# Another order of the same instructions in the repeated iteration of a two-layer attention kernel, on all five engines

## The chip, the cores and the metric

The kernel runs on one core of one Trainium2 chip. The metric is device time in microseconds (us) from launch to end, median over runs. A profiled execution also has a span, from its first to its last instruction, which is a little shorter than its time.

## The reference, cut to what matters

For each of 32 batch entries `x` (128 channels x 512 positions) and `ctx` (the same shape), two layers:

```
# layer 0: position attention, 512 x 512 energies, divided by column sums
energy = (w_qk @ ctx).T @ (w_qk @ x);  a = softmax(energy, -1);  a = a / (1e-7 + a.sum(1))
x_r = (w_v @ x + b_v) @ a
x1  = x + relu(w_t @ (x - x_r) + b_t)
# layer 1: grouped-query attention, 128 x 128 scores, 32 query heads, 8 key heads of 16
q, k, v = x1 @ Wq + bq, ctx @ Wk + bk, ctx @ Wv + bv
p = softmax(q k.T / 4 + mask);  out = (p v) @ Wo + bo
y = layernorm(out + x1) * gamma + beta
```

Everything is float32. The mask given is zero, and a flag computed at run time lets the kernel leave out its additions.

## The kernel before, in words

The batch is worked in 16 pairs; `j` (0, 1) is the entry within a pair. To keep float32 accuracy at the matmul rate of the rounded format, an operand is split in a high part (`..h`) and a low part (`..l`), and a product is three matmuls (high x high, high x low, low x high). The high part is written by ScalarE, or by GpSimd for `xs` and `ys`; the low part by VectorE or GpSimd.

The pairs are software-pipelined in four stages. Iteration `i` holds stage 0 of pair i+1 (`z_project`: the Gram matrix of `w_qk` times x), stage 1 of pair i (layer 0, and keys and values), stage 2 of pair q = i-1 (queries, maxima, scores, exponentials, weighted values) and stage 3 of pair i-2 (output projection, layer norm, store). Iterations 1, 2 and 15 run the same function `iteration` with some stages left out, 3 to 14 are a hardware loop with all of them; "a turn" below is one pass of that loop. Iteration 0 and the tail of the last pair have functions of their own.

Each engine's order of instructions is written out by hand in its own `iteration`, one for SyncE's DMA queue (from L471), GpSimd (L681), TensorE (L958), ScalarE (L1269) and VectorE (L1673). Engines meet only at counting semaphores: `wait(engine, name, i, n)` waits for the n-th signal of that name in iteration i. An instruction behind a waiting one on its engine waits too.

The 8 PSUM banks form a ring. `WIDE_USES` lists the uses of an iteration in TensorE's order (72 places, two of them "skip", so 9 times round), and a use gets the bank that the use 8 places before it had; `wait_slot` makes TensorE wait for the signal in `RELEASE` that says that use has been read. So moving a use in the order also changes whose reader it waits for. The names: `en` energies, `tva` the two layer-0 projections of x, `b` the attended sums, `z`, `q`, `k`, `v`, `vt` (transposed v), `mx` (scores from which the row maxima are taken), `m` (the maxima spread), `st` (transposed scores), `o` (weighted values), `r` (x1 transposed for the residual), `wo` (output projection).

The part that couples the engines most closely runs once per turn:

1. TensorE's four `max_scores` (L895) follow the four `q_project` (L871 to L873). VectorE reads each of the 16 banks with one `score_max` (L1567), then `max_split` (L1577 to L1582) writes `mrow`.
2. TensorE's `max_spread` (L910) turns `mrow` into bank `m`, VectorE's `max_rows` (L1588) copies it into `mrep`, and a DMA (`stack_maxima`, L413) puts it into `qstack` rows 96 and up.
3. TensorE's first `scores` (L924) waits for that DMA (`maxrow_in`), since the maxima are subtracted by the matmul itself.

SyncE issues in this stretch: 8 transfers of `qh` (L403) when the fourth `q_high` is done, 4 of `ql` (L407), the load of the next `ys` (`next_y`, L377), then the one of `mrep`. Later in the iteration stand the load of `et` (`next_et`, L383), the gathering of softmax denominators and values across partitions (L420, L425), the stores (L393), 12 transfers of `kstack` (`stack_k`, L434), and at the head of the next iteration the loads of `xt` (L380) and `xs` (L374).

At the end of an iteration VectorE inverts the denominators (`inverse_denominators`, L1592), weighs (`weigh_out`, L1598) and finishes layer 0 for j = 1 (`layer0_out`: L1531, L1534, four of L1537 and one of L1543, which writes `x2` and waits for TensorE's `residual_transpose` of the pair before, L881, for it reads the old `x2`). `x2_high` (ScalarE, L1205) and `x2_low` (GpSimd, L669) split it for the queries of the next iteration.

## Time and profile before

| what | value |
|---|---|
| median of 3 runs | 782.83 us (782.27 to 787.34) |
| profiled execution, its own time | 782.72 us |
| its span | 780.3 us |
| mean granted TensorE clock | 0.980 |
| TensorE matmul busy | 716.9 us, 92% |
| VectorE busy | 608.3 us, 78% |
| ScalarE busy | 463.5 us, 59% |
| GpSimd busy | 582.2 us, 75% |
| DMA | 101.64 MB, queue 1 takes 43.6% of 16 engines |

Busy shares tell how full an engine is, not which one sets the end. For that one reads the chain of waits (what released the last instruction, and what released that one, back to the start), and the instructions in order of time around each wait. A wait is shown at the engine that waited, with the instruction or DMA whose signal came last. For DMAs the queue's rows give the time of issue only; from issue to landing is read from the chain.

### The profile page before, as it was taken

How to read it: one execution, taken by the hardware profiler on the slowest of the kernel's cores; microseconds unless marked ns; L12 is line 12 of the kernel's file. 1: busy time of each engine (PE TensorE's matmuls, PEld its weight loads, DVE VectorE, ACT ScalarE, POOL GpSimd, SP SyncE). 2: the span in 40 equal slices, each digit the busy share in tenths (PEclk: the TensorE clock that was granted, in tenths of full speed). 3: DMA queues.
4: the chain of work that ended last, by engine and by line, in shares of the span. 5: the costliest groups of instructions: out<-in, count | busy, mean ns of one | idle time of the engine just before them, and what ended most of it. 6: DMA issues, size and time to landing. Idle time of an engine off the chain costs nothing.

```text
span 780.3 us, 17141 instructions
## 1 busy us (share of the span) xinstructions
PE 716.9 (92%) x4886; PEld 579.4 (74%) x4886; DVE 608.3 (78%) x1030; ACT 463.5 (59%) x1058; POOL 582.2 (75%) x752
## 2 busy tenths in 40 slices
PE   6798979999999999999999999999999999998773
PEld 5676867888788787878778787877878787775642
DVE  5675875969789796969879696978879697885747
ACT  5655638376574937657483855747385665748161
POOL 4886488697877969787896978789697878858054
PEclk9999999999999999999999999999999999999896
DMA  8544361634527262452717254362715436251511
GB/s 321 176 123 125 92 177 55 177 99 148 138 94 191 83 179 89 152 142 89 205 68 184 88 157 129 101 191 74 200 66 171 122 116 170 81 146 61 136 37 61
DMA packets 60363, 101.64 MB, mean 130 GB/s; under 512 B 10032, under 2 KB 30128, under 8 KB 60208
## 3 DMA queue, kind: packets, MB, share of 16 engines
q1 hardware_dynamic: 59616, 101.03, 43.6%
q10 hardware_dynamic: 720, 0.27, 0.2%
q8 instruction: 14, 0.23, 0.1%
q14 instruction: 13, 0.11, 0.0%
HBM read 41.50 MB, written 8.39 MB: 64 GB/s over the span
## 4 chain that ended last, share of the span: by engine, by line
PE 66%; DVE 12%; DMA 9%; issue 5%; SPq 3%; POOL 2%; ACT 1%; DVEq 1%; POOLq 0%; ACTq 0%
PE banks L924 8%; PE banks L840 7%; DMA qstack<-mrep 7%; DVE maxima L1567 6%; PE banks L937 5%; PE banks L871 4%; PE banks L873 4%; PE banks L872 4%; PE banks L895 4%; PE banks L827 2%; PE banks L825 2%; PE banks L826 2%; PE banks L813 2%; SPq L403 2%; PE banks L949 2%
## 5 line engine op out<-in xcount | busy, mean ns | idle before, releaser
L1567 DVE TENSOR_REDUCE maxima<-banks 128x4 f32<-128x512 f32 x256 | 158.9, 685 | 5.9 <-PE banks L895 4.5
L1226 ACT ACTIVATE prob<-banks 128x512 f32<-128x512 f32 x256 | 135.1, 608 | 26.3 <-PE banks L924 25.0
L1592 DVE RECIPROCAL dens<-dens 128x512 f32<-128x512 f32 x30 | 100.4, 3348 | 46.6 <-DMA dens<-sides 46.6
L601 POOL TENSOR_TENSOR ta<-ta,cb_s 128x516 f32<-128x516 f32 x64 | 77.1, 1205 | 74.9 <-ACT ta L1168 74.8
L840 PEld LDWEIGHTS banks<-ta,att 128*128 128x128 f32 x1024 | 119.0, 190 | 2.7 <-POOL ta L608 0.2
L840 PE MATMUL banks<-ta,att 128*128 128x130 f32 x1024 | 119.4, 275 | 0.0
L1160 ACT ACTIVATE att<-banks,negmax 128x512 f32<-128x512 f32 x128 | 88.7, 716 | 33.7 <-DVE negmax L1517 33.6
L1210 ACT ACTIVATE qh<-banks,bq_s 128x256 fp32r<-128x256 f32 x64 | 30.7, 480 | 104.1 <-PE banks L873 104.1
L924 PE MATMUL banks<-qstack,kstack 128*128 128x512 f32 x256 | 81.4, 422 | 9.5 <-DMA qstack<-mrep 9.2
L1517 DVE TENSOR_REDUCE negmax<-banks 128x1 f32<-128x512 f32 x128 | 85.2, 685 | 3.9 <-PE banks L827 3.7
L871 PE MATMUL banks<-x2h,wq_h 128*128 128x256 f32 x256 | 74.5, 291 | 4.1 <-POOL x2l L669 4.1
L1543 DVE SCALAR_TENSOR_TENSOR x<-ta,xt 128x512 f32<-128x512 f32 x32 | 38.4, 1199 | 44.9 <-PE banks L881 44.3
L873 PE MATMUL banks<-x2h,wq_l 128*128 128x256 f32 x256 | 72.7, 284 | 0.0
L872 PE MATMUL banks<-x2l,wq_h 128*128 128x256 f32 x256 | 72.4, 283 | 0.0
L1153 ACT ACTIVATE zh<-banks 128x512 fp32r<-128x512 f32 x32 | 19.4, 607 | 88.0 <-PE banks L804 88.0
L924 PEld LDWEIGHTS banks<-qstack,kstack 128*128 128x128 f32 x256 | 44.2, 191 | 32.1 <-issue 13.6
L937 PE MATMUL banks<-prob,v 128*32 128x512 f32 x512 | 62.0, 599 | 2.9 <-ACT prob L1226 2.9
L674 POOL TENSOR_TENSOR atl<-at,ath 128x512 fp32r<-128x512 f32 x30 | 44.8, 1494 | 26.0 <-ACT ath L1242 26.0
L871 PEld LDWEIGHTS banks<-x2h,wq_h 128*128 128x128 f32 x256 | 48.8, 191 | 6.5 <-POOL x2l L669 4.4
L949 PE MATMUL banks<-wo_h,ath 128*128 128x512 f32 x120 | 50.5, 421 | 2.5 <-POOL atl L674 1.5
L825 PE MATMUL banks<-zh,yh 128*128 128x512 f32 x128 | 51.3, 401 | 1.4 <-DVE maxima L1567 1.4
L827 PE MATMUL banks<-zh,yl 128*128 128x512 f32 x128 | 50.7, 396 | 0.0
(170 smaller groups left out, 1956.1 us busy)
## 6 DMA issues: line engine op xcount, KB each, us to landing
qstack<-qh SPq DMA_DIRECT2D x128, 128.0 KB, 2.4
xs<-in_x SPq DMA_DIRECT2D x16, 512.0 KB, 4.4
ys<-in_ctx SPq DMA_DIRECT2D x16, 512.0 KB, 3.8
et<-in_ctx_turned SPq DMA_DIRECT2D x16, 512.0 KB, 3.3
xt<-in_x_turned SPq DMA_DIRECT2D x16, 512.0 KB, 3.6
kstack<-kph SPq DMA_DIRECT2D x128, 64.0 KB, 2.0
qstack<-ql SPq DMA_DIRECT2D x64, 128.0 KB, 2.4
out_x<-late SPq DMA_DIRECT2D x32, 256.0 KB, 2.1
```

Source lines behind the costliest of these rows:

```text
L601: nc.gpsimd.tensor_tensor(part, part, cb_s[:].unsqueeze(1).broadcast_to([P, 2, CW]), ALU.add).then_inc(sem["ta_done"], 1)
L840: last = mm(o, att[:, j, n, bass.ts(m, P)], ta[:, j, n, 0:BW], start=n == 0, stop=n == KC - 1)
L871: mm(o, wq_h[:, k, g], x2h[:, k], start=k == 0, stop=False)
L872: mm(o, wq_h[:, k, g], x2l[:, k], start=False, stop=False)
L873: last = mm(o, wq_l[:, k, g], x2h[:, k], start=False, stop=k == KC - 1)
L924: last = mm(o, kstack[:, j, 2 * p + odd], qstack[:, p, j], start=True, stop=not masked)
L937: last = mm(banks[32 * p:32 * p + 32, slot(plan, name)], v2[:, j, 2 * p + odd], prob[:, 2 * p + odd], start=True, stop=True, tile_position ...
L1160: nc.scalar.activation(att[:, j, n], banks[:, slot(plan, f"en{j}{n}")], exp_f, bias=negmax[:, j, n:n + 1], accum_out=rowsum[:, j, n:n + 1] ...
L1226: nc.scalar.activation(prob[:, 2 * p + odd], banks[:, slot(plan, f"st{j}{kv}")], exp_f).then_inc(sem["prob_done"], 1)
L1517: nc.vector.tensor_reduce(negmax[:, j, n:n + 1], banks[:, slot(plan, f"en{j}{n}")], AX.X, ALU.max, negate=True).then_inc(sem["negmax_done" ...
L1567: nc.vector.tensor_reduce(maxima[:, 0, :, p, :, g].rearrange("x o j -> x j o"), banks[:, slot(plan, f"mx{g}{p}")].rearrange("x (j o s) -> ...
L1592: nc.vector.reciprocal(dens[:], dens[:]).then_inc(sem["dinv_done"], 1)
```

## The change: the same instructions, another order

No instruction is added or taken out, and no shape, SBUF tile or semaphore changes. In the function `iteration` of each engine some calls change places, and `WIDE_USES` is written anew to follow TensorE's order, so that many uses take another bank and wait for another reader.

```diff
--- before.py
+++ after.py
@@ -77,15 +77,15 @@
...
 WIDE_USES = (
-    ("tva00", 1), ("en00", 1), ("en01", 1), ("en02", 1), ("en03", 1), ("en10", 1), ("wo0", 3), ("tva01", 1),
-    ("tva02", 1), ("q0", 2), ("q1", 2), ("mx00", 2), ("mx01", 2), ("mx02", 2), ("mx03", 2), ("tva03", 1),
-    ("q2", 2), ("tva10", 1), ("tva11", 1), ("mx10", 2), ("mx11", 2), ("mx12", 2), ("mx13", 2), ("q3", 2),
-    ("tva12", 1), ("tva13", 1), ("mx20", 2), ("mx21", 2), ("mx22", 2), ("mx23", 2), ("mx30", 2), ("mx31", 2),
-    ("mx32", 2), ("mx33", 2), ("wo1", 3), ("skip", 1), ("skip", 1), ("en11", 1), ("en12", 1), ("m", 2),
-    ("z0", 0), ("en13", 1), ("b00", 1), ("b01", 1), ("st00", 2), ("st01", 2), ("st02", 2), ("st03", 2),
-    ("st04", 2), ("k", 1), ("st05", 2), ("st06", 2), ("st07", 2), ("z1", 0), ("r0", 2), ("o00", 2), ("o01", 2),
-    ("st10", 2), ("st11", 2), ("st12", 2), ("st13", 2), ("v", 1), ("st14", 2), ("st15", 2), ("b10", 1),
-    ("b11", 1), ("st16", 2), ("r1", 2), ("st17", 2), ("o10", 2), ("o11", 2), ("vt", 1),
+    ("en00", 1), ("en01", 1), ("tva00", 1), ("tva01", 1), ("en02", 1), ("en03", 1), ("en10", 1), ("tva02", 1),
+    ("wo0", 3), ("q0", 2), ("q1", 2), ("mx00", 2), ("mx01", 2), ("mx02", 2), ("mx03", 2), ("tva03", 1), ("q2", 2),
+    ("mx10", 2), ("mx11", 2), ("mx12", 2), ("mx13", 2), ("tva10", 1), ("tva11", 1), ("q3", 2), ("tva12", 1),
+    ("tva13", 1), ("mx20", 2), ("mx21", 2), ("mx22", 2), ("mx23", 2), ("mx30", 2), ("mx31", 2), ("mx32", 2),
+    ("mx33", 2), ("wo1", 3), ("skip", 1), ("en11", 1), ("en12", 1), ("z0", 0), ("en13", 1), ("skip", 1), ("m", 2),
+    ("b00", 1), ("b01", 1), ("st00", 2), ("st01", 2), ("st02", 2), ("st03", 2), ("st04", 2), ("st05", 2), ("k", 1),
+    ("st06", 2), ("st07", 2), ("z1", 0), ("r0", 2), ("o00", 2), ("o01", 2), ("st10", 2), ("st11", 2), ("st12", 2),
+    ("v", 1), ("st13", 2), ("st14", 2), ("st15", 2), ("b10", 1), ("b11", 1), ("st16", 2), ("vt", 1), ("st17", 2),
+    ("o10", 2), ("o11", 2), ("r1", 2),
 )
...
@@ -470,33 +470,31 @@
...
                 q = i - 1
-                if s1:
-                    this_xt(i)
                 if load_next:
                     next_x(i)
+                if s1:
+                    this_xt(i)
                 if s2:
...
                     stack_maxima(q)
+                    gather_denominators(q, 0)
+                    gather_values(q, 0)
+                    gather_denominators(q, 1)
+                if s1:
+                    next_mask(i)
+                if s3:
+                    store(i - 2, 0)
+                if s2:
+                    gather_values(q, 1)
                 if load_next:
                     next_et(i)
-                if s2:
-                    gather_denominators(q, 0)
-                    gather_values(q, 0)
-                if s3:
-                    store(i - 2, 0)
-                if s2:
-                    gather_denominators(q, 1)
-                if s1:
-                    next_mask(i)
-                if s2:
-                    gather_values(q, 1)
-                if s1:
-                    stack_k(i)
                 if s3:
                     store(i - 2, 1)
+                if s1:
+                    stack_k(i)
 
...
@@ -686,16 +684,19 @@
...
                     add_bias(i, 0, 0)
-                    add_bias(i, 0, 1)
                 if s3:
...
                 if s1:
-                    scale_values(i, 0)
+                    add_bias(i, 0, 1)
                     add_bias(i, 1, 0)
-                    add_bias(i, 1, 1)
                 if split_next:
                     split_x(i + 1, 0)
+                if s1:
+                    scale_values(i, 0)
+                if split_next:
                     split_x(i + 1, 1)
+                if s1:
+                    add_bias(i, 1, 1)
                 if s3:
...
@@ -704,14 +705,14 @@
...
                     scale_values(i, 1)
-                    spread_k(i)
-                if s2:
-                    residual_bias(q, 0)
                 if s3:
                     scale_shift(i - 2, 0)
+                if s1:
+                    spread_k(i)
                 if s3 and (s1 or s2):
...
                 if s2:
+                    residual_bias(q, 0)
                     at_low(q, 0)
...
@@ -958,17 +959,16 @@
...
                 if s1:
-                    tva_project(i, plan, 0, 0)
                     energy(i, plan, 0, 0)
                     energy(i, plan, 0, 1)
+                    tva_project(i, plan, 0, 0)
+                    tva_project(i, plan, 0, 1)
                     energy(i, plan, 0, 2)
...
                     energy(i, plan, 1, 0)
+                    tva_project(i, plan, 0, 2)
                 if s3:
                     out_project(i - 2, plan, i, 0)
-                if s1:
-                    tva_project(i, plan, 0, 1)
-                    tva_project(i, plan, 0, 2)
                 if s2:
...
@@ -977,11 +977,11 @@
...
                     q_project(q, plan, i, 2)
+                    max_scores(q, plan, i, 1, masked)
                 if s1:
...
                 if s2:
-                    max_scores(q, plan, i, 1, masked)
                     q_project(q, plan, i, 3)
...
@@ -994,12 +994,12 @@
...
                     energy(i, plan, 1, 2)
-                if s2:
-                    max_spread(q, plan, i)
                 if s0:
...
                     energy(i, plan, 1, 3)
+                if s2:
+                    max_spread(q, plan, i)
                 if s1:
...
@@ -1009,10 +1009,10 @@
...
                     scores(q, plan, i, 0, 4, masked)
+                    scores(q, plan, i, 0, 5, masked)
                 if s1:
...
                 if s2:
-                    scores(q, plan, i, 0, 5, masked)
                     scores(q, plan, i, 0, 6, masked)
...
@@ -1024,10 +1024,10 @@
...
                     scores(q, plan, i, 1, 2, masked)
+                if s1:
+                    kv_project(i, plan, "v", 1, "v_ps")
+                if s2:
                     scores(q, plan, i, 1, 3, masked)
-                if s1:
-                    kv_project(i, plan, "v", 1, "v_ps")
-                if s2:
                     scores(q, plan, i, 1, 4, masked)
...
@@ -1035,12 +1035,13 @@
...
                     scores(q, plan, i, 1, 6, masked)
-                    residual_transpose(q, plan, i, 1)
+                if s1:
+                    v_transpose(i, plan)
+                if s2:
                     scores(q, plan, i, 1, 7, masked)
...
                     values(q, plan, i, 1, 1)
-                if s1:
-                    v_transpose(i, plan)
+                    residual_transpose(q, plan, i, 1)
 
...
@@ -1268,31 +1269,31 @@
...
                 q = i - 1
-                if s2:
-                    x2_high(q, 1)
+                if s1:
+                    tva_raw(i, plan, 0, 0)
+                    tva_raw(i, plan, 0, 1)
                 if weights:
                     out_weights_high()
+                if s2:
+                    x2_high(q, 1)
                 if s1:
                     exp_energy(i, plan, 0, 0)
-                    tva_raw(i, plan, 0, 0)
                     exp_energy(i, plan, 0, 1)
+                    tva_raw(i, plan, 0, 2)
                     exp_energy(i, plan, 0, 2)
...
                     exp_energy(i, plan, 1, 0)
-                    tva_raw(i, plan, 0, 1)
-                    tva_raw(i, plan, 0, 2)
                 if s2:
...
                     at_high(i - 2, 1)
+                if s2:
+                    q_high(q, plan, 2)
                 if s1:
                     tva_raw(i, plan, 0, 3)
-                if s2:
-                    q_high(q, plan, 2)
-                if s1:
                     tva_raw(i, plan, 1, 0)
...
@@ -1315,39 +1316,43 @@
...
                     exp_scores(q, plan, 0, 6)
+                if s1:
+                    k_high(i, plan)
+                if s2:
                     exp_scores(q, plan, 0, 7)
-                if s1:
-                    k_high(i, plan)
+                if s3:
+                    normalise(i - 2, 0)
+                if s2:
+                    keep_sums(q, plan, 0, 0)
                 if s0:
...
                 if s2:
-                    keep_sums(q, plan, 0, 0)
                     keep_sums(q, plan, 0, 1)
-                if s3:
-                    normalise(i - 2, 0)
-                if s2:
+                    exp_scores(q, plan, 1, 0)
                     residual(q, plan, 0)
...
                 if s2:
-                    exp_scores(q, plan, 1, 0)
                     exp_scores(q, plan, 1, 1)
                     exp_scores(q, plan, 1, 2)
+                if s3 and (s1 or s2):
+                    normalise(i - 2, 1)
+                if s1:
+                    x2_high(i, 0)
+                if s2:
                     exp_scores(q, plan, 1, 3)
                     exp_scores(q, plan, 1, 4)
-                if s3 and (s1 or s2):
-                    normalise(i - 2, 1)
-                if s2:
                     exp_scores(q, plan, 1, 5)
...
                     keep_sums(q, plan, 1, 0)
+                if s1:
+                    v_place(i, plan, 0)
+                if s2:
+                    keep_sums(q, plan, 1, 1)
                     at_high(q, 0)
-                    keep_sums(q, plan, 1, 1)
                     residual(q, plan, 1)
                 if s1:
-                    x2_high(i, 0)
-                    v_place(i, plan, 0)
                     v_place(i, plan, 1)
...
@@ -1682,12 +1687,11 @@
...
                     energy_max(i, plan, 1, 0)
+                    row_inverse(i, 0)
                 if s3:
...
                     q_low(q, plan, 0)
-                if s1:
-                    row_inverse(i, 0)
                 if s3:
...
@@ -1696,9 +1700,9 @@
...
                     score_max(q, plan, 0, 3)
-                    q_low(q, plan, 2)
                     score_max(q, plan, 1, 0)
                     score_max(q, plan, 1, 1)
+                    q_low(q, plan, 2)
                     score_max(q, plan, 1, 2)
...
@@ -1710,26 +1714,28 @@
...
                     score_max(q, plan, 3, 3)
+                if s3:
+                    residual_add(i - 2, plan, 1)
+                if s2:
                     max_split(q)
                 if s3:
-                    residual_add(i - 2, plan, 1)
                     row_statistics(i - 2, 1)
...
                     energy_max(i, plan, 1, 1)
+                if s0:
+                    z_low(i, plan, 0)
                 if s2:
                     max_rows(q, plan)
+                if s1:
+                    energy_max(i, plan, 1, 2)
                 if s3:
...
                 if s1:
-                    energy_max(i, plan, 1, 2)
                     energy_max(i, plan, 1, 3)
                     ctx_low(i)
-                if s0:
-                    z_low(i, plan, 0)
-                if s1:
-                    row_inverse(i, 1)
                     layer0_out(i, plan, 0)
                     k_low(i, plan)
+                    row_inverse(i, 1)
                 if s0:
...
```

## Rows read from the trace of the kernel before

**Rows 1.** The page: TensorE's busy time, and the chain's shares by engine.

```profile
PE 716.9 (92%) x4886; PEld 579.4 (74%) x4886; DVE 608.3 (78%) x1030; ACT 463.5 (59%) x1058; POOL 582.2 (75%) x752
...
PE 66%; DVE 12%; DMA 9%; issue 5%; SPq 3%; POOL 2%; ACT 1%; DVEq 1%; POOLq 0%; ACTq 0%
```

**Rows 2.** Windows view, one turn: length, busy us (instructions) per engine, clock, DMA, GB/s.

```profile
473.31:518.40 45.09, 43.95 (x307) 35.76 (x306) 36.85 (x61) 28.18 (x66) 36.67 (x49) 1.00 0.46 132
```

**Rows 3.** TensorE in order of time, same turn: start, us, instruction, idle before it.

```profile
477.12 1.42 PE L924 MATMUL banks<-qstack,kstack 128*128 128x512 f32 x5 [0.38 <-DMA qstack<-mrep]
...
493.19 0.36 PE L813 MATMUL banks<-cw_h,xh 128*128 128x258 f32 x1
...
500.59 0.28 PE L871 MATMUL banks<-x2h,wq_h 128*128 128x256 f32 x1
...
516.39 0.33 PE L910 MATMUL banks<-ident_r,mrow 128*128 128x128 f32 x1 [0.61 <-DVE mrow L1582]
```

**Rows 4.** Chain that ended last, same turn: start us, us, what.

```profile
473.31 3.58 DMA qstack<-mrep
...
477.12 1.42 PE banks L924 x5
...
493.43 0.12 PE banks L813
...
493.79 0.23 PE banks L825
...
503.62 0.66 PE banks L895 x8
...
511.75 3.68 DVE maxima L1567 x6
...
516.17 0.69 DVE late L1604
...
518.17 0.21 DVE mrep L1588
...
518.40 3.52 DMA qstack<-mrep
```

**Rows 5.** SyncE's queue in order of time, same turn (issue time alone).

```profile
506.05 0.35 SPq L380 DMA_DIRECT2D xt<-in_x_turned  x1
506.70 0.39 SPq L374 DMA_DIRECT2D xs<-in_x  x1
510.01 5.03 SPq L403 DMA_DIRECT2D qstack<-qh  x8
515.09 2.50 SPq L407 DMA_DIRECT2D qstack<-ql  x4
517.68 0.53 SPq L377 DMA_DIRECT2D ys<-in_ctx  x1
```

**Rows 6.** Chain, iteration 15, in which no ys is loaded.

```profile
698.99 2.48 DMA qstack<-mrep
```

**Rows 7.** VectorE in order of time, same turn as Rows 3.

```profile
477.25 0.68 DVE L1511 TENSOR_TENSOR zl<-banks,zh 128x512 fp32r<-128x512 f32 x1
...
492.04 1.13 DVE L1537 SCALAR_TENSOR_TENSOR ta<-banks,colinv,ta 128x128 f32<-128x128 f32 x4
493.20 1.58 DVE L1543 SCALAR_TENSOR_TENSOR x<-ta,xt 128x512 f32<-128x512 f32 x1
```

**Rows 8.** ScalarE in order of time, same turn.

```profile
492.27 0.60 ACT L1236 ACTIVATE sides<-banks 128x512 f32<-128x512 f32 x1 [0.43 <-PE banks L937]
...
494.76 0.58 ACT L1199 ACTIVATE v<-banks 128x64 f32<-128x64 f32 x4
```

**Rows 9.** GpSimd in order of time, same turn.

```profile
498.40 1.30 POOL L669 TENSOR_TENSOR x2l<-x,x2h 128x512 fp32r<-128x512 f32 x1
```

**Rows 10.** Chain, iteration 2.

```profile
109.57 5.00 DMA qstack<-mrep
```

**Rows 11.** SyncE's queue, iteration 2.

```profile
112.11 0.35 SPq L383 DMA_DIRECT2D et<-in_ctx_turned  x1
```

More of the change, by code:

```diff
@@ L472, in iteration @@
                 q = i - 1
+                if load_next:
+                    next_x(i)
                 if s1:
                     this_xt(i)
-                if load_next:
-                    next_x(i)
                 if s2:
@@ L490, in iteration @@
                 if s2:
-                    gather_denominators(q, 1)
-                if s1:
-                    next_mask(i)
-                if s2:
                     gather_values(q, 1)
+                if load_next:
+                    next_et(i)
+                if s3:
+                    store(i - 2, 1)
                 if s1:
                     stack_k(i)
-                if s3:
-                    store(i - 2, 1)
             def first_iteration(i, load_next, s1, s2, s3, setup=False):
@@ L1026, in iteration @@
                     scores(q, plan, i, 1, 2, masked)
-                    scores(q, plan, i, 1, 3, masked)
                 if s1:
@@ L1030, in iteration @@
                 if s2:
+                    scores(q, plan, i, 1, 3, masked)
                     scores(q, plan, i, 1, 4, masked)
@@ L1295, in iteration @@
                 if s1:
+                    tva_raw(i, plan, 0, 3)
                     tva_raw(i, plan, 1, 0)
```

9 lines of the change are left out of this document (3 added, 6 removed).

## The prediction

> **What bounds the kernel now.** I read the page first. TensorE is busy 92% of the span and has 66% of the chain of waits; the next is VectorE with 12%, then DMA with 9% [rows 1]. So TensorE is near the bound, and the question is what its remaining waits hang on. Then one turn of the loop: it takes 45.09 us, of which TensorE is busy 43.95 [rows 2]. At most 1.14 us a turn can be won by order alone, 13.7 us over 12 turns. TensorE in order of time shows where most of it lies: 0.61 us ahead of `max_spread`, which waits for `mrow`, and 0.38 us ahead of the first `scores`, which waits for the transfer of `mrep` [rows 3].
>
> The chain shows which of these repeats the turn. From the first scores at 477.12 it stays on TensorE to the first `max_scores` at 503.62, then runs through VectorE's 16 maxima, `residual_add`, `max_rows`, and ends in the transfer of `mrep`, 3.52 us, after which the next scores begin [rows 4]. SyncE's queue gives a second road to the same place: 8 issues of `qh` from 510.01 (5.03 us), 4 of `ql` (2.50 us), `ys` at 517.68, and only behind it `mrep` at 518.40 [rows 4, 5]. The queue starts that series when the fourth query projection has been copied, so this road too starts at TensorE and ends at `mrep`.
>
> Which road binds is told by the transfer itself. Issued at 473.31 it takes 3.58 us [rows 4]. In iteration 15, where no `ys` goes ahead of it, it takes 2.48 us [rows 6]. The 1.10 us between them is time behind `ys`. The landing is thus set by when `ys` was issued, and `mrep` could be issued up to about 1.1 us later for the same landing.
>
> **The change part by part.** The sum goes against the profiled execution's own 782.72 us, 0.11 us under the median of 782.83, so no correction is needed.
>
> *TensorE, `max_spread` behind `z_project` 0 and `energy(1,3)`.* Six matmuls of 512 columns, 0.23 us apart [rows 4], or 1.4 us, now fill the 0.61 us wait [rows 3]; the wait ahead of `max_spread` goes. But TensorE reaches the scores that much earlier and they still wait for `mrep`. If the landing stays, the 0.38 us becomes 0.99 us and the turn keeps its length: 0.
>
> *VectorE, `z_low` 0 ahead of `max_rows`; `residual_add` 1 ahead of `max_split` instead of behind it.* `residual_add` already stands between the last maximum and `max_rows`, at 516.17 [rows 4], so `mrep` does not see it; only `mrow` comes 0.69 us later, and TensorE has the 1.4 us to cover that. `z_low` is new on this path: 0.68 us [rows 7]. So `mrep` is issued at most 0.68 us later. Bounds: nothing, if the landing hangs on `ys` (1.10 us of slack, 0.42 left), and +0.68 x 12 = +8.2 us if the transfer's time runs from its own issue. I take 0, since rows 4 and 6 are the same transfer with and without `ys` ahead. Below nothing is excluded: even an earlier `mrep` would be behind `ys`.
>
> The Trainium skill speaks against this, in "DMA: Bandwidth & Descriptors", "Anatomy of one DMA": a DMA costs a fixed time of about 2 us plus its bytes over a bandwidth, counted from its issue. By that the later issue would be paid in full. The trace disagrees with a fixed cost here, 3.58 against 2.48 us for the same bytes.
>
> *SyncE, `xs` ahead of `xt`, `et` and one store ahead of the 12 `stack_k`.* The queue gets the issue of one 512 KB load (0.35 to 0.39 us plus a gap) ahead of `stack_k`, so `xs` and `xt`, issued at 506.70 and 506.05 now [rows 5], end some 0.4 us later as a pair, while `xs` alone is first. The queue then still waits for `qh` at 510.01, 2.9 us after the last of them: hidden. What could leak is their data being in the way of `qh`; bounds 0 and +0.4 x 12 = +4.8 us. I take 0, the queue's pause being far longer.
>
> *The seam between iterations.* TensorE now begins with `en00` where `tva00` stood at 493.19, and `en00`, `en01` take the banks of `b10`, `b11`. VectorE frees these with the four L1537 at 492.04, lasting 1.13 us [rows 7]: the second half at 492.6, the last at 493.17, needed at 493.19 and 0.69 us later. ScalarE's tail is reordered: `v_place` ended at 495.34 and had `x2_high` 0 ahead of it, which is moved 6 places up; the tail from `keep_sums` at 492.27 loses that 0.5 us and ends near 494.8 [rows 8]. `tva01` wants the bank of `vt` from it, at 493.19 + 1.39 + 0.36 = 494.94. Margins of 0.1 to 0.5 us where there were 0.5 us and more. `residual_transpose` 1 now ends the iteration; `x2` for j = 1, at 493.20 [rows 7], waits for it, and it ends at about 493.3. Then `x2_low` ends at 499.70 [rows 9] and the queries start at 500.59 [rows 3], a slack of 0.9 us that swallows small delays. Bounds: 0 and +0.7 us a turn (the `v_place` tail as late as now, 495.34, plus its signal and the delayed `x2`); nearest row is 494.8, so I take +0.1 over 13 turns: +1.3 us.
>
> *The rest* (`max_scores` 1 ahead of two `tva`, `k_high`, `normalise`, `scale_values`, `spread_k`, `row_inverse` 1, `v` one score earlier) moves work between places where the chain never passes. The sum of TensorE's work from the scores to `max_scores` 0 is the same set of matmuls. VectorE's maxima are then served no earlier. Cost 0; cover is ScalarE's and GpSimd's idle time (28.18 and 36.67 us busy of 45.09 [rows 2]); without it, up to one `score_max` or copy, 0.7 us a turn.
>
> *`et` out from behind `mrep`.* In iteration 2 `mrep` takes 5.00 us [rows 10], and the load of `et` is issued at 112.11 while it is under way [rows 11]; in the turns `mrep` takes 3.58 [rows 4]. The change puts `et` far later. Bounds 0 and -1.42 us there; iteration 1 is alike with a third of that. I take -1.4 in all, near the row. In the turns `et` follows the landing of `mrep`, and nothing is won.
>
> Sum: 782.7 + 0 + 0 + 1.3 - 1.4 = 782.6 us; I say 782.
>
> **The rivals.**
>
> *A, slower: the later `mrep` is paid.* Place: the wait of the first scores. Price 0.68 x 12 = 8.2 us, less the `et` gain: 789.5 us, and with the leak of `xt` up to 792. It decides from the point where VectorE is more than 1.1 us later than now; a late `z_high` ahead of `z_low` would do it. For: `mrep` was issued just when VectorE had it ready (518.17 + 0.21 against 518.40 [rows 4]). Against: rows 6. Chance 0.13.
>
> *B, slower: the seam.* `v_place` 1 stands behind `residual` 1, which waits for the last matmuls of the iteration; if that tail is 0.8 us later than I place it, `tva01` stops TensorE by 0.7 us: 13 x 0.7 = 9.1 us, 791 us. It decides from 0.1 us. For: thin margins. Against: ScalarE waits at 492.27 [rows 8], so the tail is short of work, not late. Chance 0.14.
>
> *C, faster: the freed wait is won.* If the landing of `mrep` moved with TensorE, the 0.61 us would be won: 0.61 x 12 = 7.3 us, and 1.4 at the start: 774.0 us. It needs the queue's series to start earlier, by smoother work ahead of the fourth query projection. Against: TensorE has no wait listed between the scores and `max_scores` 0, the chain being all matmuls there [rows 4]. Chance 0.15.
>
> *D: all is hidden*, my forecast, 0.58: 779 to 786 us.
>
> **How the numbers follow.** The likeliest case gives 782. From no change a measurement of this kernel can tell about 1%, 7.8 us: below 775.0 or above 790.7. Faster by that: most of C, 0.13. Slower: half of A, most of B, 0.19. Between: D, the rest of the others and unnamed small effects, 0.68. The range leaves out the lower part of C and the upper ends of A and B: 774 to 791.
>
> **What would show it.** Right, if in the changed kernel's turn the idle ahead of `max_spread` is gone, the idle ahead of the first scores is about 1.0 us, `mrep` is issued about 0.6 us later in the turn and takes about 2.9 us instead of 3.5, and the turn stays at 45.1 us. A would show as a transfer of still 3.5 us and a turn of 45.7; B as a wait of `en` or `tva` at the head of the turn for ScalarE or VectorE; C as a turn of 44.5 with the fourth query projection earlier after the scores. In iteration 2 `mrep` should take about 3.6 us. Wrong is the forecast if the turn moves by more than 0.3 us either way.

## The result, and the profile after

The changed kernel takes 788.01 us (median of 8 runs, 786.22 to 790.69), the kernel before 782.57 us (8 runs, 782.14 to 787.34). The ratio is 1.0057, with a 95% interval of 1.0034 to 1.0081: 5.4 us slower, inside the range of the forecast and under its bound of 1%, but it moved where the forecast said that it would not, and by more than the measurement is uncertain. The profiled execution took 789.49 us, with a span of 787.6 us.

The page of the changed kernel; the last field of the line beginning with L925 is the idle time ahead of that group of instructions and what ended it:

```profile
span 787.6 us, 17111 instructions
PE 719.1 (91%) x4886; PEld 584.2 (74%) x4886; DVE 598.9 (76%) x1030; ACT 467.6 (59%) x1058; POOL 580.8 (74%) x752
...
PE 67%; DVE 11%; DMA 9%; issue 6%; POOL 3%; SPq 2%; ACT 1%; DVEq 1%; POOLq 0%
...
L925 PE MATMUL banks<-qstack,kstack 128*128 128x512 f32 x256 | 81.4, 424 | 23.3 <-DMA qstack<-mrep 23.3
```

The chain's shares have hardly moved against [rows 1]. What has moved is the wait ahead of the scores: 23.3 us over 15 waits, where the kernel before has 9.2 us. Part of it is no new wait: the 0.61 us a turn that stood ahead of `max_spread` [rows 3] now stands here.

First the loop's steady part, in the turn that answers to [rows 2, 3]. TensorE in order of time, and the windows view of the same turn:

```profile
521.17 0.40 PE L828 MATMUL banks<-zh,yl 128*128 128x512 f32 x1
521.41 0.22 PE L911 MATMUL banks<-ident_r,mrow 128*128 128x128 f32 x1
521.47 3.79 PE L841 MATMUL banks<-ta,att 128*128 128x130 f32 x32
526.50 1.61 PE L925 MATMUL banks<-qstack,kstack 128*128 128x512 f32 x6 [1.24 <-DMA qstack<-mrep]
```

```profile
core 0: us, PE busy (x) PEld busy (x) DVE busy (x) ACT busy (x) POOL busy (x), PEclk, DMA share, GB/s
481.53:526.50 44.97, 43.71 (x306) 35.77 (x306) 35.83 (x61) 28.48 (x65) 36.54 (x48) 1.00 0.46 133
```

`max_spread` (L911) follows its neighbour with no wait, the scores wait 1.24 us instead of 0.38, and the turn is 44.97 us long against 45.09. Over the turns 5 to 14 the wait is 1.13 to 1.59 us, so this is one of the shorter ones, and the turns are 45.13 us long on average, against 45.10. The chain of waits shows `z_low` now in front of `max_rows`, and SyncE's queue shows `ys` where it was:

```profile
522.26 0.68 DVE zl L1516
522.94 0.21 DVE mrep L1593
...
523.17 3.08 DMA qstack<-mrep
```

```profile
522.09 0.53 SPq L377 DMA_DIRECT2D ys<-in_ctx  x1
523.17 0.64 SPq L413 DMA_DIRECT2D qstack<-mrep  x1
```

From the first scores `ys` is issued after 40.56 us in both kernels (477.12 to 517.68 [rows 3, 5], 481.53 to 522.09 here). `mrep` is issued 1.08 us behind `ys` instead of 0.72, and lands 4.16 us after the issue of `ys` instead of 4.24 (518.40 + 3.52 less 517.68 [rows 4, 5]). The later issue is paid back by the shorter transfer.

So the loss is not in the steady turn. The table cuts the span at the landings of `mrep` (issue plus transfer time in each chain of waits). Iteration n's landing is the end of that transfer in iteration n; the last column but one is the last pair's landing, in the tail. The two lower rows are repeats of both kernels in one later session, described as experiments below.

| kernel | landing, iteration 1 | 1 to 4 | 4 to 14 | 14 to 15 | 15 to last pair | rest | span |
|---|---|---|---|---|---|---|---|
| before | 67.0 | 139.4 | 451.0 | 44.1 | 41.9 | 36.9 | 780.3 |
| changed | 69.9 | 140.5 | 451.3 | 44.5 | 44.2 | 37.2 | 787.6 |
| before, repeated | 67.1 | 135.3 | 451.2 | 44.2 | 42.3 | 37.3 | 777.5 |
| changed, repeated | 68.8 | 142.0 | 451.9 | 43.7 | 43.3 | 37.4 | 787.0 |

The ten turns that make up 57% of the span differ by 0.3 and 0.7 us. The rest is in the first iteration (+2.9, +1.7), the next three (+1.1, +6.7) and the last pair (+2.3, +1.0). One profile of each kernel can't give these shares: the same kernel differs from itself by up to 4.1 us in iterations 1 to 4.

**Iteration 1.** ScalarE of the changed kernel in order of time, then the same engine of the kernel before:

```profile
44.06 0.88 ACT L1169 ACTIVATE ta<-banks 128x258 f32<-128x258 f32 x2 [4.94 <-PE banks L816]
44.83 1.91 ACT L1268 ACTIVATE wo_h<-prob 128x2048 fp32r<-128x2048 f32 x1
46.64 0.62 ACT L1206 ACTIVATE x2h<-x 128x512 fp32r<-128x512 f32 x1
```

```profile
38.37 0.63 ACT L1205 ACTIVATE x2h<-x 128x512 fp32r<-128x512 f32 x1 [0.28 <-DVE x L1543]
38.90 1.89 ACT L1267 ACTIVATE wo_h<-prob 128x2048 fp32r<-128x2048 f32 x1
```

TensorE of the changed kernel, where its instructions of iteration 1 begin and where the queries begin:

```profile
40.62 0.62 PE L826 MATMUL banks<-zh,yh 128*128 128x512 f32 x1 [4.01 <-issue]
...
48.71 0.38 PE L872 MATMUL banks<-x2h,wq_h 128*128 128x256 f32 x1 [1.77 <-POOL x2l L667]
```

In iteration 1 TensorE starts its function late, after 4.01 us of issue (3.21 us in the kernel before). The changed ScalarE puts two `tva_raw` and the copy `wo_h` ahead of `x2_high` 1; the `tva_raw` have to wait for TensorE, so `x2_high` falls from 38.37 to 46.64. GpSimd's `x2_low` follows at 47.39, and the queries wait 1.77 us for it. In the steady turn the queries show no such wait.

**Iterations 2 to 4.** The waits of the changed TensorE ahead of the first scores in iterations 1 to 4, and the windows view behind the first, the second and around the third of them (the clock is the third field from the right):

```profile
70.12 1.75 PE L925 MATMUL banks<-qstack,kstack 128*128 128x512 f32 x6 [1.94 <-DMA qstack<-mrep]
117.47 1.62 PE L925 MATMUL banks<-qstack,kstack 128*128 128x512 f32 x6 [2.26 <-DMA qstack<-mrep]
163.64 2.88 PE L925 MATMUL banks<-qstack,kstack 128*128 128x512 f32 x6 [2.36 <-DMA qstack<-mrep]
210.66 1.62 PE L925 MATMUL banks<-qstack,kstack 128*128 128x512 f32 x6 [1.73 <-DMA qstack<-mrep]
```

```profile
71.30:74.70 3.40, 3.40 (x16) 3.14 (x16) 0.00 (x0) 2.37 (x5) 2.60 (x3) 0.53 0.02 5
...
117.47:161.28 43.81, 43.77 (x305) 35.73 (x305) 33.65 (x55) 28.01 (x64) 34.01 (x42) 1.00 0.46 136
161.28:163.64 2.36, 0.00 (x2) 0.03 (x1) 2.27 (x7) 0.58 (x2) 1.93 (x6) 1.00 0.14 39
163.64:167.10 3.46, 3.46 (x10) 2.90 (x11) 0.00 (x0) 2.60 (x6) 3.03 (x7) 0.51 0.01 2
```

These waits of 1.73 to 2.36 us stand against 1.13 to 1.59 us in the steady turns. Behind the one of 2.36 us the granted clock is 0.51 for 3.46 us, its lower level of 1.2 GHz, which costs some 1.7 us more (an estimate: 3.46 x 0.49). The wait of 1.94 us is followed, 1.18 us later, by such a stretch too, and the one of 2.26 us by none: the length of a wait alone doesn't tell whether the clock falls. The Trainium skill ("TensorE: Matmul & The Clock Gate", section "HAM oscillation — how this bites in real kernels") tells of a kernel whose clock falls back again and again where TensorE waits for DMA. The trace agrees in part: the waits of 1.94 and 2.36 us for `mrep` are such places, the one of 2.26 us is not. Why the landing is late there is in part in the transfer. The chain of waits of the changed kernel, `mrep` of iterations 2, 3 and 5, then the same of the repeat of the kernel before:

```profile
113.08 4.15 DMA qstack<-mrep
...
159.20 4.20 DMA qstack<-mrep
...
252.30 3.08 DMA qstack<-mrep
```

```profile
108.30 3.82 DMA qstack<-mrep
...
153.56 3.65 DMA qstack<-mrep
...
243.84 3.58 DMA qstack<-mrep
```

**The end.** In iteration 15 ScalarE's `at_high` 0 now stands behind `keep_sums` 1. GpSimd waits for it, and its `x2_low` and TensorE's queries of the last pair come behind (GpSimd first, then TensorE):

```profile
723.15 1.27 POOL L672 TENSOR_TENSOR atl<-at,ath 128x512 fp32r<-128x512 f32 x1 [1.32 <-ACT ath L1243]
```

```profile
728.15 0.58 PE L872 MATMUL banks<-x2h,wq_h 128*128 128x256 f32 x1 [4.34 <-POOL x2l L667]
```

The queries start 21.95 us after the landing at 706.20, where the kernel before has 21.19 (701.47 [rows 6] to 722.66). The order of iteration 15 thus costs 0.76 us up to the queries. The rest of the 2.3 us lies behind them, and there the clock differs. The windows view from the first of these queries on (722.66 and 728.15), of the kernel before and then of the changed one:

```profile
722.00:726.00 4.00, 3.34 (x17) 3.34 (x18) 2.35 (x2) 0.37 (x1) 0.61 (x1) 0.57 0.35 89
726.00:730.00 4.00, 4.00 (x38) 3.73 (x38) 2.87 (x6) 1.06 (x3) 0.00 (x0) 1.00 0.38 95
```

```profile
726.00:730.00 4.00, 1.85 (x8) 1.85 (x9) 3.27 (x2) 0.00 (x0) 2.09 (x2) 0.61 0.54 179
730.00:734.00 4.00, 4.00 (x26) 3.68 (x24) 0.48 (x1) 0.80 (x2) 0.00 (x0) 0.54 0.42 107
```

From the landing of iteration 15 to the last pair's the granted clock averages 0.91 in the kernel before (0.87 in its repeat, with 42.3 us) and 0.85 in the changed one (0.84 in its repeat, with 43.3 us). `e1_x2_first`, described below, has the changed order in iteration 15 and an average of 0.91; it takes 42.7 us, 0.8 more than the kernel before at the same clock. So some 0.8 us of the end go with the order. The rest comes with the lower clock in these profiles, and whether the order makes that likelier isn't shown.

### The profile page after: what moved, and what is told of

The parts are those of the page before. It is cut to its first block, busy times and chain, and to the rows that moved or that the text cites. A ratio compares the mean times of both kernels' runs of the same rounds, so it can differ in the third digit from the quotient of the medians.

```text
span 787.6 us, 17111 instructions
## 1 busy us (share of the span) xinstructions
PE 719.1 (91%) x4886; PEld 584.2 (74%) x4886; DVE 598.9 (76%) x1030; ACT 467.6 (59%) x1058; POOL 580.8 (74%) x752
## 4 chain that ended last, share of the span: by engine, by line
PE 67%; DVE 11%; DMA 9%; issue 6%; POOL 3%; SPq 2%; ACT 1%; DVEq 1%; POOLq 0%
PE banks L925 8%; PE banks L841 7%; PE banks L938 7%; DMA qstack<-mrep 6%; DVE maxima L1572 6%; PE banks L872 4%; PE banks L873 4%; PE banks L874 4%; PE banks L896 3%; PE banks L814 3%; PE banks L826 2%; PE banks L950 2%; PE banks L828 2%; PE banks L827 2%; PE banks L952 2%
## 5 line engine op out<-in xcount | busy, mean ns | idle before, releaser
L672 POOL TENSOR_TENSOR atl<-at,ath 128x512 fp32r<-128x512 f32 x30 | 40.7, 1358 | 91.6 <-ACT ath L1243 91.5
L1161 ACT ACTIVATE att<-banks,negmax 128x512 f32<-128x512 f32 x128 | 87.1, 686 | 34.4 <-DVE negmax L1522 34.1
L925 PE MATMUL banks<-qstack,kstack 128*128 128x512 f32 x256 | 81.4, 424 | 23.3 <-DMA qstack<-mrep 23.3
L1548 DVE SCALAR_TENSOR_TENSOR x<-ta,xt 128x512 f32<-128x512 f32 x32 | 32.7, 1023 | 73.7 <-PE banks L882 73.6
L925 PEld LDWEIGHTS banks<-qstack,kstack 128*128 128x128 f32 x256 | 45.1, 193 | 43.9 <-issue 39.2
L1169 ACT ACTIVATE ta<-banks 128x258 f32<-128x258 f32 x128 | 47.7, 386 | 19.7 <-PE banks L816 19.4
```

What stands on the lines that cost most here:

```text
L925: last = mm(o, kstack[:, j, 2 * p + odd], qstack[:, p, j], start=True, stop=not masked)
L1161: nc.scalar.activation(att[:, j, n], banks[:, slot(plan, f"en{j}{n}")], exp_f, bias=negmax[:, j, n:n + 1], accum_out=rowsum[:, j, n:n + 1] ...
```

## The experiments

The theory at the outset: the steady turn hangs on `ys` and on TensorE as forecast, and the loss is in the iterations outside it. The rival: a turn's joined wait of 1.1 to 1.6 us, now in one piece, is itself the loss, through the clock. The trace of the changed kernel already speaks against it in the steady turns, where the granted clock stays at 1.00 from 220 to 700 us of the span. All ratios are to the kernel before, from five rounds, with 95% intervals.

### Which part of the program carries the loss

`e1_x2_first` brings `x2_high` 1 and the copy of the weights back to the head of iteration 1.

```
+                if weights:
+                    x2_high(q, 1)
+                    out_weights_high()
                 if s1:
...
-                if weights:
-                    out_weights_high()
-                if s2:
+                if s2 and not weights:
                     x2_high(q, 1)
```

> The changed kernel, with one edit in iteration 1 alone: ScalarE's x2_high(0, 1) and the copy of Wo stand ahead of the two tva_raw again. Edge theory (the loss is in the iterations outside the loop): the first transfer of mrep lands at about 67 us of the span instead of 69.7, and the time falls by about 2.7 us, to 785.3 from 788.0, perhaps by more where the clock falls less often. Loop theory (a later mrep is paid in every turn): the edit touches no turn, and the time stays at 788.

Measured: 786.15 us, 1.0047 (1.0022 to 1.0071). `mrep` of iteration 1 lands at 67.3 instead of 69.9 us, and from TensorE's start of iteration 1 the queries come after 6.17 us (40.09 to 46.26) instead of 8.09 (40.62 to 48.71). The kernel before has 6.21 in its repeat (39.68 to 45.89). So in iteration 1 this order is what delays the queries. When TensorE starts that iteration differs between profiles (39.5 to 43.4 us), so its own part is seen best from that start: the landing comes 27.1 to 27.6 us after it in the five profiles with `x2_high` 1 first and `ys` ahead of `mrep` (the kernel before and its repeat, `e1_x2_first`, `e2_loop_only`, `e7_x2_at`), and 28.7 to 29.3 us in five with the changed order there (the changed kernel and its repeat, `e3_edges_only`, `e6_rows_first`, `e10_sync_old`). The time gives back less than the intervals tell apart (1.0047 against 1.0057), and iterations 1 to 4 stay long, 138.5 us.

`e2_loop_only` keeps the changed order in iterations 2 to 14 and gives iterations 1 and 15 the order and the ring of before; `e3_edges_only` is the reverse.

```
+EDGE_WIDE_USES = (      # the ring of the other kernel, for iterations 1 and 15
...
+            edge_iteration(1, SECOND, True, True, True, False)
...
+            edge_iteration(PAIRS - 1, NEXT_TO_LAST, False, True, True, True)
```

> Iterations 1 and 15 in the order of the kernel before on all five engines, with its ring of banks there; iterations 2 to 14 in the changed order. Edge theory: the loss of the changed kernel goes nearly whole, 782 to 784 us, and turns of 45.1 us. Loop theory: all but the two edge iterations' share of the loss stays, 787 us or more.

> The reverse: iterations 1 and 15 in the changed order, 2 to 14 as in the kernel before. Edge theory: most of the loss is here, 785 to 788 us. Loop theory: under 784 us.

Measured: 786.17 us, 1.0045 (1.0023 to 1.0066), for the loop alone, and 784.54 us, 1.0031 (1.0003 to 1.0059), for the edges alone. The two excesses, 0.45% and 0.31%, make 0.76% together, against 0.57% and 0.73% measured for the whole change. Neither theory had this: each put nearly all of the loss on one side, and both sides have a part. Which is larger the intervals don't tell, and the one of the edges reaches almost to 1. In the profile of the edges alone the ten turns 4 to 14 take 451.3 us and the turns 1 to 4 take 135.7, as in the repeat of the kernel before; what remains is iteration 1 (69.7) and the last pair (44.2). With the loop alone the turns 1 to 4 take 139.7 us, with these waits:

```profile
116.19 1.62 PE L1006 MATMUL banks<-qstack,kstack 128*128 128x512 f32 x6 [3.23 <-DMA qstack<-mrep]
162.69 2.90 PE L1006 MATMUL banks<-qstack,kstack 128*128 128x512 f32 x6 [2.74 <-DMA qstack<-mrep]
```

So the loop's loss comes with the new order of iterations 2 to 4 themselves and is not handed on by iteration 1. The loop alone has its first landing at 69.4 us; its queries come 6.22 us after TensorE's start, as before, but the start is at 41.83.

### Does one of the five orders carry it

`e9_spread_back` takes `max_spread` back between `energy(1,2)` and `z_project` 0, with the ring to match, so the wait is split in two again.

```
                     energy(i, plan, 1, 2)
+                if s2:
+                    max_spread(q, plan, i)
                 if s0:
...
                     energy(i, plan, 1, 3)
-                if s2:
-                    max_spread(q, plan, i)
```

> The changed kernel with TensorE's max_spread back ahead of z_project 0 and energy(1,3), and the ring with it: one long wait ahead of the first scores is cut in two again, one ahead of max_spread and one ahead of the scores. Theory (in iterations 1 to 4 the joined wait of 2.2 to 3.2 us is followed by a stretch at the lower clock): no wait above 2 us from iteration 2 on, fewer such stretches before 200 us of the span, turns 2 to 4 together 137 us or less instead of 140.5, turns 5 to 14 unchanged at 45.1 us each; 786 us or less. Rival (the joining costs nothing, the landing alone counts): turns 2 to 4 stay near 139 to 140 us, time 788 us; if the spread is late through z_low's wait for z_high, more than that.

Measured: 789.14 us, 1.0073 (1.0053 to 1.0094). The theory of this expectation failed, and its rival (the landing alone counts) has the time about right: the loss doesn't come from the joining. The turns 1 to 4 take 141.3 us, the turns 4 to 14 even 453.7, 2.4 more than with the changed kernel. In iteration 2 both waits are there, 0.97 us ahead of `max_spread` and 2.04 us ahead of the scores, with a stretch at the lower clock behind. In a steady turn nothing is split: TensorE waits 1.11 us ahead of `max_spread` and not at all ahead of the scores.

`e10_sync_old` gives SyncE the whole order of before (`xt` ahead of `xs`, `et` behind `mrep`, both stores where they were).

```
-                if load_next:
-                    next_x(i)
                 if s1:
                     this_xt(i)
+                if load_next:
+                    next_x(i)
...
                     stack_maxima(q)
+                if load_next:
+                    next_et(i)
...
```

> The changed kernel with SyncE's order of the kernel before; the other engines as changed. The forecast gave SyncE's part a gain of 1.4 us at the start (et no longer beside mrep) and no loss: without it the time would be 1 to 2 us more than the changed kernel's 788, turns 5 to 14 at 45.1 us. Rival (the moved loads are in the way of the qh and ys transfers): turns 2 to 4 shorter than 138 us and a time of 785 us or less.

Measured: 790.25 us, 1.0095 (1.0071 to 1.0119). The changed kernel of the same session has 1.0073 (1.0045 to 1.0101), so the intervals overlap. SyncE's new order is not the loss; it may gain 1 or 2 us, which these intervals don't settle. The turns 1 to 4 take 141.1 us.

`e6_rows_first` puts VectorE's `max_rows` ahead of `z_low` again, so that `mrep` is ready 0.68 us earlier.

```
-                if s0:
-                    z_low(i, plan, 0)
                 if s2:
                     max_rows(q, plan)
+                if s0:
+                    z_low(i, plan, 0)
```

> The changed kernel with VectorE's max_rows ahead of z_low again, so that mrep is ready 0.6 us earlier; ys is still issued ahead of it. Forecast's reading: the transfer is issued 0.6 us earlier, takes that much longer behind ys, and the turn stays at 45.1 us. Rival A (a later mrep is paid): turns of 44.5 us and 7 us less time.

Measured: 787.34 us, 1.0073 (1.0041 to 1.0105), the turns 4 to 14 at 451.6 us: no gain, as the theory has it. The 0.68 us on VectorE is free while `ys` goes first.

`e7_x2_at` is the first edit and, in iteration 15 alone, `at_high` 0 ahead of `keep_sums` 1.

```
                 if s2:
+                    if not s0:
+                        at_high(q, 0)
                     keep_sums(q, plan, 1, 1)
-                    at_high(q, 0)
+                    if s0:
+                        at_high(q, 0)
```

> The changed kernel with two edge edits on ScalarE: x2_high(0, 1) first in iteration 1, and at_high ahead of the last keep_sums in iteration 15. Edge theory: the first mrep lands at 67 us of the span, and in the last pair the scores-to-scores stretch loses some 0.5 us against the changed kernel beside what the clock does; near 784.5 us. Rival (the end is the clock alone): the end of iteration 15 is not shorter.

Measured: 787.10 us, 1.0045 (1.0015 to 1.0074), not told apart from the first edit alone at 1.0047. `mrep` of iteration 1 lands at 69.1 us and not at 67, because TensorE starts late (42.00 us); counted from there it is 27.1 us, as it should be. From the landing of iteration 15 to the last pair's it takes 43.7 us, against 42.7 with the first edit alone and 44.2 in the changed kernel. The edit at the end is a miss: from the first scores of iteration 15 the queries come after 21.53 us (703.59 to 725.12), against 21.70 in the changed kernel and 20.95 in the one before. So `at_high` explains 0.17 of the 0.75 us. The second `x2` of VectorE is ready 0.5 us later there in both; which of the moved calls does that isn't shown.

### Is ys what the turn hangs on

`e4_before_y_late` is the kernel before and `e5_after_y_late` the changed one, each with SyncE's `stack_maxima` ahead of `next_y`.

```
                     stack_q(q)
+                if s2:
+                    stack_maxima(q)
                 if load_next:
                     next_y(i)
                 if s2:
-                    stack_maxima(q)
                     gather_denominators(q, 0)
```

> The kernel before, with one edit on SyncE's queue: the load of the next ys is issued behind the transfer of mrep instead of ahead of it. Theory that mrep's landing hangs on ys ahead of it: issue to landing falls from 3.5 to about 2.5 us, TensorE's idle time ahead of the first scores (0.38 us) goes, and the turn shortens by what TensorE idles there, to 44.7 us; 778 us or a little less, since the wait for mrow (0.61 us) stays. Rival, a fixed cost from its own issue: the transfer still takes 3.5 us, the turn stays at 45.1 and the time at 782.6 us.

> The changed kernel with ys issued behind mrep on SyncE's queue, nothing else. In the kernel before that edit made the transfer short (2.6 us) and left the turn at 45.1 us, because the fifth scores then waited for the bank that z_low frees, behind GpSimd's variance. The changed order has z_low ahead of all that. Theory of two roads, each closed by the other: now both are open, TensorE's idle ahead of the first scores falls from 1.2 to about 0.8 us, the turn is 44.6 to 44.8 us, and the sum of turns 4 to 14 falls by 3 to 5 us. Rival (the turn is bound elsewhere, or the transfer is not shortened): turns of 45.1 us.

Measured: 782.23 us, 0.9989 (0.9971 to 1.0006), for the kernel before, and 775.53 us, 0.9920 (0.9893 to 0.9947), for the changed one. The same edit is worth nothing in the one order and some 11 to 12 us in the other (from 1.0057 and 1.0073 to 0.9920). By the profiles 4.8 us of these are in the ten steady turns (451.3 to 446.5), 4.5 us below the kernel before, and 6.4 us in iterations 1 to 4 (140.5 to 134.1), where they mostly take back the changed kernel's own loss. TensorE of the first, the two waits of the turn that is 45.1 us long, and its chain of waits between them:

```profile
467.17 0.32 PE L910 MATMUL banks<-ident_r,mrow 128*128 128x128 f32 x1 [0.60 <-DVE mrow L1582]
473.87 0.49 PE L924 MATMUL banks<-qstack,kstack 128*128 128x512 f32 x1 [0.33 <-DVE zl L1511]
```

```profile
467.67 0.70 DVE bns L1609
...
470.37 0.21 POOL nv L644
...
471.39 0.68 DVE negmax L1517
472.07 0.96 DVE x2l L1549
...
473.14 0.68 DVE zl L1511
...
473.87 0.49 PE banks L924
```

With `ys` out of the way no scores wait for `mrep`. Another wait is there at once: the layer norm's root on GpSimd (L637 to L644), a VectorE that waits for it, and `z_low` behind it, whose bank the fifth scores need. Two roads set the turn of the kernel before at the same 45.1 us. The changed order has `z_low` ahead of `max_rows` and of that stretch, and gives the fifth scores another bank. The new ring hands the bank of `z0` to the third scores, two earlier than before, so it is the place of `z_low` and not the ring that should open the road; no run has the one without the other, so this is argued from the order and not shown. With `mrep` ahead of `ys` its chain of waits goes through `mrep` and no longer over that road:

```profile
515.24 0.21 DVE mrep L1594
...
515.46 2.62 DMA qstack<-mrep
```

The transfer takes 2.62 us instead of 2.98 to 3.43, and turns 4 to 14 take 446.5 us. The Trainium skill ("DMA: Bandwidth & Descriptors", section "Queues, rings and completion order") says that an engine takes descriptors in the order of the ring; the trace agrees, since the same 64 KB takes 0.4 to 0.8 us less where 512 KB don't stand ahead. Turns 1 to 4 take 134.1 us: the long waits there go too (0.89, 0.78 and 0.76 us in iterations 2 to 4), and no stretch at the lower clock is left before 220 us of the span. So the landing was late there through `ys` standing ahead of `mrep`.

`e8_best` joins this with `e6` and `e7`.

> The changed kernel with all of these: ys behind mrep, max_rows ahead of z_low, and both edge edits. Theory of two roads: mrep is issued at the time of the kernel before and takes 2.6 us, the fifth scores do not wait for z_low, and the turn nears TensorE's busy 43.95 us plus little: 44.0 to 44.4 us; 12 turns give 8 to 13 us, so 770 to 776 us. Rival: a third road at 45.1 us and a time of 780 us or more.

Measured: 771.49 us (771.15 to 773.13), 0.9868 (0.9843 to 0.9893): 11.4 us faster than the kernel before, 16.5 faster than the changed one. `max_rows` first, worth nothing behind `ys`, now pays, the ten turns going from 446.5 to 444.3 us; the edge edits don't touch these turns. Its page:

```profile
span 771.2 us, 17111 instructions
PE 723.1 (94%) x4886; PEld 580.0 (75%) x4886; DVE 593.9 (77%) x1030; ACT 468.0 (61%) x1058; POOL 587.5 (76%) x752
...
PE 84%; DVE 4%; DMA 3%; POOL 3%; issue 2%; SPq 2%; ACT 1%; DVEq 0%; POOLq 0%
```

and the windows view of two turns (88.84 us from first scores to first scores) and a little more:

```profile
423.80:513.00 89.20, 88.79 (x612) 71.49 (x613) 71.85 (x123) 57.34 (x132) 74.42 (x97) 1.00 0.46 136
```

TensorE has 84% of the chain where it had 66% [rows 1], and 88.79 of 89.20 us are busy: in the turn this version is at TensorE's own work.

### How sure are the stages of the table

`e11_before_again` and `e12_after_again` are the two kernels without an edit, with the experiments of the last session.

> The kernel before, unchanged, for a second trace on this chip. Edge theory: first mrep landing 65 to 67 us, turns 5 to 14 at 45.1 us each, and turns 2 to 4 at 135.5 us where no wait above 2 us and no lower clock falls in them, against 139.4 in the first trace, which had one.

> The changed kernel, unchanged, for a second trace on this chip. Edge theory: first mrep landing near 70 us, turns 2 to 4 near 139 us with waits above 2 us and a stretch at the lower clock, turns 5 to 14 at 45.1 us each, last pair near 44 us; some 5 us over the kernel before.

Measured: 784.03 us, 1.0003 (0.9979 to 1.0027), and 788.95 us, 1.0073 (1.0045 to 1.0101). The loss of the change repeats. Iterations 1 to 4 of the kernel before do not: 139.4 us in the first profile, with one wait of 3.30 us in iteration 2, and 135.3 in the second, where that wait is 0.80:

```profile
112.37 1.40 PE L924 MATMUL banks<-qstack,kstack 128*128 128x512 f32 x5 [0.80 <-DMA qstack<-mrep]
```

The changed kernel has long waits there in both (2.26 and 2.36 us, and 2.48 and 2.57 in the repeat), as every kernel with its loop and `ys` first: 138.5 to 142.0 us in eight profiles, the three with one piece of the old order (`e6`, `e9`, `e10`) among them, against 135.3 to 135.7 in three of the four with the old loop. The lower clock is a part of it: between the first landing and the fourth there are two such stretches in the changed kernel, three in its repeat and one or two in each of the other six, none in the three short ones and one in the long profile of the kernel before, each worth some 1.7 us (an estimate, as above).

The late landing is the other part. In iteration 2 two things add up: `ys` is issued 41.73 us after the scores (70.12 to 111.85), where the steady turn has 40.56, and `mrep` lands 5.38 us behind it (117.23), where the steady turn has 4.16. The stretch at clock 0.53 lies between those scores and `ys` and may be what delays it, but the first profile of the kernel before has 41.65 us there without one. In iteration 3 `ys` is in time (117.47 to 158.14, 40.67 us) and its `mrep` still lands 5.26 us behind it, against 4.37 in the old order (152.84 to 157.21). What slows the load of `ys` in the second and third iteration of the new order isn't shown; it stays open.

## Why the prediction was wrong, point by point

- *The steady turn.* Right in its points: no idle ahead of `max_spread`; idle ahead of the scores 1.13 to 1.59 us, with about 1.0 forecast; `mrep` issued 0.36 us later after the scores, with 0.6 forecast, and taking 2.98 to 3.43 us, with 2.9 forecast; the turn unchanged, 45.1 us on average over the ten (451.3 / 10).
- *`z_low` ahead of `max_rows`, taken at 0 (rival A at 8.2 us).* Right while `ys` goes first, by `e6_rows_first` and by the equal landing behind `ys`. Ten turns at 451.3 us against 451.0 leave no room for 0.68 us in each. The Trainium skill's fixed time counted from the issue ("DMA: Bandwidth & Descriptors", "Anatomy of one DMA", a section on transfers that GpSimd issues, where SyncE issues these) would have made an estimated 6.8 us of it over ten turns; the measurement decides against it for this queue.
- *The seam, +1.3 us over 13 turns, and rival B.* The forecast's 0.1 us a turn makes 1.0 over ten turns; the turns 4 to 14 show +0.3 and +0.7 us in all, so it was a little large. No `en` or `tva` waits at the head of the turn. (The price of B is 782.7 + 9.1 - 1.4 = 790.4 us, not 791.)
- *The step that failed: "The rest ... moves work between places where the chain never passes", taken at 0.* It was worked out from rows of the steady turn, and multiplied by turns; iterations 1 and 15 had no term of their own. They run the same functions with other engines late, and there the chain does pass. The move of `x2_high` 1 behind two `tva_raw` isn't even in the list of *the rest*; the nearest is the seam's "a slack of 0.9 us that swallows small delays" ahead of the queries. In iteration 1 the queries wait 1.77 us instead, and come 1.7 to 1.9 us later from TensorE's start (8.09 and 7.87 against 6.21), which `e1_x2_first` takes back. At the end the order costs 0.75 us up to the queries, of which `at_high` is 0.17 by `e7_x2_at`. `e3_edges_only` puts the edges at 0.31% of the time, 2.4 us.
- *The other half, in iterations 2 to 4.* "If the landing stays, the 0.38 us becomes 0.99 us and the turn keeps its length" holds where the landing comes as in the steady turn, and I took it for all of the loop. In iterations 2 and 3 of the new order `mrep` lands 5.38 and 5.26 us behind the issue of `ys` instead of 4.16, TensorE waits 2.26 and 2.36 us, and some of these waits have the lower clock behind them. I had no term for the clock. `e2_loop_only` puts this part at 0.45%, 3.5 us. `e5_after_y_late`, in which these waits are under 0.9 us, shows that it takes `ys` ahead of `mrep`; why the landing is later there than in the same iterations of the old order stays open.
- *`et` out from behind `mrep`, -1.4 us.* Not borne out. The row it rests on, 5.00 us in iteration 2 [rows 10], was one execution's. In the repeat of the same kernel the transfer takes 3.82 us and has landed (112.12) when `et` is issued (112.15), so the two don't meet there. The changed kernel has 4.15 us with no `et` near, where 3.6 was forecast. What made the 5.00 us isn't shown.
- *What the forecast missed on the other side.* "At most 1.14 us a turn can be won by order alone" [rows 2] was right, but it took one road for the turn, the one through `ys`. `e4_before_y_late` shows a second at the same length. The worth of the change lies in opening that second road, and it shows only once the first is open as well: 0.9920, and 0.9868 with `max_rows` first and the two edge edits. That `z_low`'s place does it is argued above and not tested alone.

## What to carry to other kernels

An order that is written once for a pipelined loop also runs in the filling and draining iterations; cost it there by their own rows, above all where one engine starts late and another has instructions ahead that wait for it. When an edit moves a wait and the time stays, look for a second road of the same length before calling the edit worthless, and try both edits together. A single long wait in one profile should be seen in a second execution before a term is made of it.

## What the runs showed of the hardware that was not expected

A wait of TensorE of 2.36 us was followed by 3.46 us at a granted clock of 0.51, one of 1.94 us by 3.40 us at 0.53, and one of 2.26 us by none, while the waits of 1.13 to 1.59 us in the steady turns left it at 1.00. In the last pair the same order of instructions had an average clock of 0.91 in one profile (`e1_x2_first`) and 0.85 in another (the changed kernel). A transfer of 64 KB behind a load of 512 KB on one queue took 2.98 to 3.43 us in the steady turns, 4.15 and 4.20 in iterations 2 and 3 of the same execution, and 2.62 with the load behind it.
